# Taking the integer rounding of a normalised tile from eight compare-and-subtract rounds on one engine to eight relu/min rounds on two halves and two engines

## The reference, cut to what matters

```
xn    = layernorm(x)
query = xn@Wq ; key = xn@Wk ; value = xn@Wv
gq    = sum_s(query * softmax(query*SCALE))        # over the sequence
gk    = sum_s(p * softmax(p*SCALE)),  p = gq*key
attn  = query + (gk*value) @ Wr
ffn   = bitlinear(silu(bitlinear(xn, w_gate)) * bitlinear(xn, w_up), w_down)
out   = x + attn + ffn
_act_quant(x): scale = 127/max|x| per row; xq = clip(round(x*scale), -128, 127)/scale
_weight_quant(w): scale = 1/mean|w|; wq = clip(round(w*scale), -1, 1)/scale
```

## Time and profile before

| | us |
|---|---|
| median of 2 runs (5271.18 and 5273.79) | 5272.49 |
| profiled execution, its own time | 5271.05 |
| its span, first to last instruction, slowest core (the eight: 5258.3 to 5269.4) | 5269.4 |
| busy in the span: PE / DVE / ACT / POOL | 2267.0 / 3306.7 / 1899.7 / 60.7 |
| batch 0, after its first loads (125 to 640) | 515 |
| between the batches (640 to 796) | 156 |
| batch 1 (796 to 1378) | 582 |
| pass B (1378 to 1905) | 527 |
| gate/up stage (1905 to 4265) | 2360 |
| down projection (4265 to 5269) | 1004 |

### The profile page before, as it was taken

How to read it: one execution, slowest core, us unless ns; L and a number is a source line. 1 busy time by engine, 2 the same in 40 slices (tenths; PEclk the granted TensorE clock), 3 DMA queues, 4 the chain that set the end, 5 groups by cost and what they waited for, 6 DMA issues and landing times.

```text
span 5269.4 us, 37071 instructions; the slowest of 8 cores (5258.3 to 5269.4 us)
## 1 busy us (share of the span) xinstructions
PE 2267.0 (43%) x9998; PEld 1013.2 (19%) x10182; DVE 3306.7 (63%) x3647; ACT 1899.7 (36%) x2114; POOL 60.7 (1%) x117
## 2 busy tenths in 40 slices
PE   1443313433200043444444444444444406888888
PEld 0111101111100011211112111121111103444443
DVE  3777657777557767777777777777777731111111
ACT  1222213333100026555565655556555521111111
POOL 1000000000000000000000000000000000000000
PEclk9666656666555567767777677776767757888888
DMA  4222203333233310000000000000000032222221
GB/s 83 77 78 73 73 0 104 106 102 102 76 113 117 116 50 20 20 20 11 20 20 21 16 15 21 20 20 11 19 20 20 16 88 92 90 84 83 90 86 52
DMA packets 85712, 296.02 MB, mean 56 GB/s; under 512 B 9728, under 2 KB 9728, under 8 KB 77312
## 3 DMA queue, kind: packets, MB, share of 16 engines
q1 hardware_dynamic: 32256, 134.23, 7.3%
q10 hardware_dynamic: 39168, 117.46, 6.5%
q0 software_dynamic: 14080, 41.95, 3.1%
HBM read 209.72 MB, written 92.27 MB: 57 GB/s over the span
## 4 chain that ended last, share of the span: by engine, by line
DVE 38%; PE 27%; ACT 17%; issue 9%; DMA 7%; DVEq 1%; ACTq 1%; another core or an unknown queue 0%; POOL 0%; SPq 0%; POOLq 0%
ACT rA L666 10%; DVE fl L669 9%; PE PB L607 6%; DVE lh L360 6%; PE PC L610 6%; PE PA L807 4%; PE PC L807 4%; DVE lh L357 3%; PE PB L793 3%; DVE stat L628 3%; PE PT L777 2%; ACT z_hqT L781 2%; DVE fl L675 2%; DMA wdT_sb<-swdT 2%; ACT f_g L616 2%
## 5 line engine op out<-in xcount | busy, mean ns | idle before, releaser
L607 PE MATMUL PB<-wgT_sb,f_xiT 128*128 128x512 bf16 x1962 | 827.6, 422 | 1239.8 <-ACT f_g L616 1204.0
L666 ACT ACTIVATE rA<-fl,cbias 128x1024 bf16<-128x1024 f32 x512 | 588.1, 1149 | 440.0 <-DVE fl L656 284.9
L669 DVE SCALAR_TENSOR_TENSOR fl<-rA,fl 128x1024 f32<-128x1024 bf16 x512 | 627.2, 1225 | 163.2 <-ACT rA L666 162.9
L675 DVE SCALAR_TENSOR_TENSOR fl<-rB,fl 128x1024 f32<-128x1024 bf16 x512 | 625.0, 1221 | 15.1 <-ACT rB L672 13.0
L672 ACT ACTIVATE rB<-fl,cbias 128x1024 bf16<-128x1024 f32 x512 | 586.9, 1146 | 17.1 <-DVE fl L675 15.2
L607 PEld LDWEIGHTS PB<-wgT_sb,f_xiT 128*128 128x128 bf16 x2048 | 217.6, 106 | 1575.2 <-issue 1387.3
L610 PE MATMUL PC<-wuT_sb,f_xiT 128*128 128x512 bf16 x1024 | 468.0, 457 | 3.6 <-issue 2.4
L610 PE MATMUL PA<-wuT_sb,f_xiT 128*128 128x512 bf16 x1024 | 389.6, 380 | 18.3 <-DVE f_h L619 15.9
L616 ACT ACTIVATE f_g<-PB,cgv 128x512 f32<-128x512 f32 x256 | 168.0, 680 | 542.7 <-PE PC L610 530.8
L360 DVE TENSOR_TENSOR lh<-lh,lh 128x1024 f32<-128x1024 f32 x256 | 313.7, 1225 | 27.3 <-DVE lh L357 0.9
L470 PE MATMUL P<-p_w,p_rep 128*128 128x512 bf16 x62 | 36.3, 585 | 601.4 <-DVE p_w L467 553.9
(11 more groups left out here) (126 smaller groups left out, 3400.3 us busy)
## 6 DMA issues: line engine op xcount, KB each, us to landing
shqT<-f_hq SPq DMA_DIRECT2D x32, 1024.0 KB, 4.4
z_hq<-shqT SPq DMA_DIRECT2D x32, 1024.0 KB, 6.9
wf<-wgT ACTq DMA_DIRECT2D x48, 512.0 KB, 3.6
wf<-wuT ACTq DMA_DIRECT2D x48, 512.0 KB, 3.5
wf<-wdT ACTq DMA_DIRECT2D x48, 512.0 KB, 3.5
xbuf<-x SPq DMA_DIRECT2D x32, 512.0 KB, 4.1
sacc<-accs SPq DMA_DIRECT2D x32, 512.0 KB, 2.9
z_acc<-sacc ACTq DMA_DIRECT2D x32, 512.0 KB, 7.9
```

Of the source, the lines that this page charges most:

```text
L607: last = te.matmul(gps, lhsT, wgT_sb[:, k * I + jj * 512:k * I + (jj + 1) * 512], start=(k == 0), stop=(k == 7))
L666: o("scalar", (lambda j=j, scale=scale: lambda s: s.activation(rA[:], fl1[:], AF.Relu, scale=scale, bias=cbias[:, j:j + 1]))(), reads=[fl1 ...
L669: o("vector", (lambda cc=cc, op1=op1: lambda v: v.scalar_tensor_tensor(fl1[:], rA[:], cc, fl1[:], ALU.min, op1))(), reads=[rA_b], writes=[ ...
L675: o("vector", (lambda cc=cc, op1=op1: lambda v: v.scalar_tensor_tensor(fl2[:], rB[:], cc, fl2[:], ALU.min, op1))(), reads=[rB_b], writes=[ ...
```

## The change

In `stB` the rounding is rewritten, in the form that the gate/up stage has already. The tile is cut into two halves of 512 columns, lh1 and lh2, each made by a tensor_scalar of its own. A round is now, per half, a relu on ScalarE (2^40 times the difference to the power of two, so that the result is zero or very large; lrA or lrB, bf16) and a min-and-subtract on VectorE. The first round leaves the sum with its sign turned, so the later ones use the negative factor and add; in the end lh1 and lh2 hold minus the fraction. Two scalar_tensor_tensor make x*scale minus the fraction into xi16, and one tensor_scalar adds 0.5 in place. The biases `cbias` exist already (L255 to L258). The changed kernel's lines below this point lie 2 to 19 lower.

```diff
-    lh1, lh1_b = sb("lh1", [128, D], F32, 149.125)
-    lh2, lh2_b = sb("lh2", [128, D], F32, 153.125)
+    lh1, lh1_b = sb("lh1", [128, 512], F32, 149.125)
+    lh2, lh2_b = sb("lh2", [128, 512], F32, 151.125)
+    lrA, lrA_b = sb("lrA", [128, 512], BF16, 153.125)
+    lrB, lrB_b = sb("lrB", [128, 512], BF16, 154.125)
...
-        o("vector", (lambda t=t: lambda v: v.tensor_scalar(
-            lh1[:], xnf[:], svec[:, t:t + 1], 128.5, ALU.mult, ALU.add))(),
+        hA = xnf[:, 0:512]
+        hB = xnf[:, 512:1024]
+        o("vector", (lambda t=t, hA=hA: lambda v: v.tensor_scalar(
+            lh1[:], hA, svec[:, t:t + 1], 128.5, ALU.mult, ALU.add))(),
           reads=[xnf_b, svec_b], writes=[lh1_b])
-        for kb in range(7, -1, -1):
-            cc = float(2 ** kb)
-            o("vector", (lambda cc=cc: lambda v: v.tensor_scalar(
-                lh2[:], lh1[:], cc, cc, ALU.is_ge, ALU.mult))(),
-              reads=[lh1_b], writes=[lh2_b])
-            o("vector", lambda v: v.tensor_tensor(lh1[:], lh1[:], lh2[:], ALU.subtract),
-              reads=[lh2_b], writes=[lh1_b])
-        o("vector", (lambda t=t: lambda v: v.tensor_scalar(
-            lh2[:], xnf[:], svec[:, t:t + 1], 0.5, ALU.mult, ALU.add))(),
+        o("vector", (lambda t=t, hB=hB: lambda v: v.tensor_scalar(
+            lh2[:], hB, svec[:, t:t + 1], 128.5, ALU.mult, ALU.add))(),
           reads=[xnf_b, svec_b], writes=[lh2_b])
-        o("vector", lambda v: v.tensor_tensor(xi16[:], lh2[:], lh1[:], ALU.subtract),
-          reads=[lh2_b, lh1_b], writes=[xi16_b])
+        for j in range(8):
+            cc = float(2 ** (7 - j))
+            scl = (2.0 ** 40) if j == 0 else -(2.0 ** 40)
+            op1 = ALU.subtract if j == 0 else ALU.add
+            o("scalar", (lambda j=j, scl=scl: lambda s: s.activation(
+                lrA[:], lh1[:], AF.Relu, scale=scl, bias=cbias[:, j:j + 1]))(),
+              reads=[lh1_b, cbias_b], writes=[lrA_b])
+            o("vector", (lambda cc=cc, op1=op1: lambda v: v.scalar_tensor_tensor(
+                lh1[:], lrA[:], cc, lh1[:], ALU.min, op1))(),
+              reads=[lrA_b], writes=[lh1_b])
+            o("scalar", (lambda j=j, scl=scl: lambda s: s.activation(
+                lrB[:], lh2[:], AF.Relu, scale=scl, bias=cbias[:, j:j + 1]))(),
+              reads=[lh2_b, cbias_b], writes=[lrB_b])
+            o("vector", (lambda cc=cc, op1=op1: lambda v: v.scalar_tensor_tensor(
+                lh2[:], lrB[:], cc, lh2[:], ALU.min, op1))(),
+              reads=[lrB_b], writes=[lh2_b])
+        o("vector", (lambda t=t, hA=hA: lambda v: v.scalar_tensor_tensor(
+            xi16[:, 0:512], hA, svec[:, t:t + 1], lh1[:], ALU.mult, ALU.add))(),
+          reads=[xnf_b, svec_b, lh1_b], writes=[xi16_b])
...
+        o("vector", lambda v: v.tensor_scalar_add(xi16[:], xi16[:], 0.5),
+          reads=[xi16_b], writes=[xi16_b])
```

More of the change, by code:

```diff
@@ new lines, in stB @@
+        o("vector", (lambda t=t, hA=hA: lambda v: v.scalar_tensor_tensor(
+            xi16[:, 0:512], hA, svec[:, t:t + 1], lh1[:], ALU.mult, ALU.add))(),
+          reads=[xnf_b, svec_b, lh1_b], writes=[xi16_b])
+        o("vector", (lambda t=t, hB=hB: lambda v: v.scalar_tensor_tensor(
+            xi16[:, 512:1024], hB, svec[:, t:t + 1], lh2[:], ALU.mult, ALU.add))(),
+          reads=[xnf_b, svec_b, lh2_b], writes=[xi16_b])
+        o("vector", lambda v: v.tensor_scalar_add(xi16[:], xi16[:], 0.5),
+          reads=[xi16_b], writes=[xi16_b])
```

## The result

| | us |
|---|---|
| kernel before, median of 10 runs | 5291.93 |
| changed kernel, median of 13 runs | 5545.08 |
| ratio, 95% interval | 1.0461 (1.0415 to 1.0507) |
| profiled execution of the changed kernel, its own time | 5498.03 |
| predicted time and range | 5450 (5400 to 5500) |

The ratio leaves out runs in which one die ran at a lower granted clock, and the medians contain them, so the ratio and the profiled executions (5271.05 and 5498.03, +227 us) are what to compare. The changed kernel is slower, as forecast, by more than forecast: +227 us against +179. Its profiled execution lies 2 us inside the range; the ratio, 1.0461 x 5271 = 5514 us, and the median lie outside it.

What follows compares the result with a forecast made beforehand. VectorE was taken to bound both batches, with pass A hidden beside its rounding. Exposing pass A gave +39 us in batch 0 and +126, +18 and -4 in batch 1: +179 on 5271.05, so 5450 us, range 5400 to 5500.

Steps and rivals of the forecast that it cites:

- What bounds the kernel, and why pass A costs nothing there: Both batches: VectorE leads; pass A lies beside its 19.90 us rounding, with 6.22 us of cover left.
- The new rounding by itself: Rounding in the batches: a round takes 1.68 us, and VectorE saves 3.8 us per tile.
- The head: Start of the new rounding, a tensor_scalar of 512 columns on VectorE: 0.42 us.
- The tail: End of the rounding, after the last subtraction: second scalar_tensor_tensor 0.75 us, addition of 0.5 0.55 us; ends at about 16.1.
- What it moves: Batch steps: pass A's first load waits for the last relu, 15.4 us later; steps grow 2.8 and 9.66 us.
- The third term: Step path, pass A from first load issue to key copy: 8.7 us in batch 0, 15.6 in batch 1.
- The second term: Step path, from the rounding's start to the start of the last relu: 12.98 us.
- The sum: Whole kernel: +39 us in batch 0, +126, +18 and -4 in batch 1, together +179 us.
- The advice to keep relu on VectorE: Skill's rule for the rounding's relus: the swap loses by 1.66 times the time per element, whatever lies beside it.
- Hidden pass A: Rival, batch steps: pass A stays hidden and VectorE's gain comes through, -118 us, 5155 us; chance 0.03.
- Another table: Rival, ScalarE: relus need another table than Ln and Exp, +80 us on top, 5532 us; chance 0.03.
- Shrinking waits: Rival, pass A's loads: only a step's first sum waits, so +27 us, 5298 us; chance 0.04.

Runs made afterwards that it cites:

- run 4: Kernel before, with all 96 pieces of pass A moved out of the steps to behind batch 1; 5631.83 us.
- run 8: Kernel before, with pass A's loads issued two pieces ahead; ratio to the kernel before 0.9976.
- run 1: Changed kernel, with the store of the integer tile held back until the next step's sum x + query is written; median 5487.07 us, ratio 1.0404.
- run 3: Changed kernel, with all 96 pieces of pass A moved out of the steps to behind batch 1; 5552.55 us.
- run 7: Changed kernel, loads issued two pieces ahead, three pass A pieces a step in both batches, two behind the exponent, one behind the relus; ratio 0.9816.
- run 2: Changed kernel, with each of pass A's loads issued two pieces ahead, behind the sum that frees its buffer; median 5336.8 us, ratio 1.0122.

## Why the prediction was right or wrong

**What bounds the kernel, and why pass A costs nothing there: right.** Run 4, without pass A, and run 8, with early loads, leave the step at 35.24 to 35.27 us.

**The new rounding by itself: right in its rounds, short in its tail.** The relu has 0.722 us (0.72 expected), the subtraction 0.692 (0.69), a round is 1.68 us, and in most steps the last relu starts 12.97 us after the rounding's start (12.98). In 9 of 27 steps on core 7 it starts some 0.3 us later, which gives means of 13.12 in batch 0 and 13.05 in batch 1. The head has 0.49 (0.42) and the addition of 0.5 took 0.43 (0.55 taken, 0.25 to 0.75 the bounds). The tail left out an instruction: L378 (0.74 us) stands behind the last subtraction in VectorE's list too, and the prediction counted only the second of the two that make xi16. So the rounding lasts 16.52 us where no round is late, not 16.1, and VectorE gains 3.4 us per tile, not 3.8. This cost the sum nothing, since the tail lies beside pass A.

**What it moves: right.** The load is issued when the last relu starts, the step's path is reciprocal, rounding, pass A, key copy, exponent; VectorE waits at the reciprocal 15.6 to 17.8 us in batch 1 (15 predicted) and 8.3 to 9.7 in batch 0 (8). The gap from key copy to reciprocal is 1073.56 - 1069.54 = 4.02 us (4.04).

**The third term, pass A from first issue to key copy, was sized too small, and this is the step that failed.** The four terms of a step, as means over the steps 3 to 16 of batch 0 and 3 to 15 of batch 1, from the timelines of two cores of the changed kernel:

| us | reciprocal to rounding | to last relu | pass A | key copy to reciprocal | step |
|---|---|---|---|---|---|
| batch 0, predicted | 12.31 | 12.98 | 8.7 | 4.04 | 38.0 |
| batch 0, core 7 (slowest) | 12.33 | 13.12 | 9.42 | 4.04 | 38.90 |
| batch 0, core 6 (fastest) | 12.33 | 13.12 | 8.98 | 4.04 | 38.46 |
| batch 1, predicted | 12.31 | 12.98 | 15.6 | 4.04 | 44.9 |
| batch 1, core 7 | 12.37 | 13.05 | 17.24 | 4.02 | 46.68 |
| batch 1, core 6 | 12.37 | 13.05 | 16.49 | 4.02 | 45.93 |

The other three terms stand. Pass A was put 0.72 and 1.64 us too low for the slowest core; over 14 and 15 steps this makes 10 + 25 = 35 of the 48 us that are missing. The second term adds 3 us, the first reciprocal of batch 0 came 4 us later on this core (131.82 instead of 127.62), and 6 us lie behind the last reciprocal of batch 1, in stages that the change does not touch. Three things are in the 35:
- *In batch 1 the row came from a core with short loads.* Core 6 was the slowest before, when nothing of its loads counted. Its mean from issue to sum in batch 1 was 3.60 us, the lowest of the eight; their mean was 3.74 and the highest 3.86. (In batch 0, from step 2 on, core 6 had 3.80 against a mean of 3.72, so this does not explain batch 0.) In the changed kernel core 6 is the fastest of all, and the slowest core decides:

```profile
core 6: 5471.0 us, clock 0.701
core 7: 5496.4 us, clock 0.702
```

- *The store of the integer tile runs into the second load*, +0.4 us, which run 1 took away: 12 us over the two batches.
- *A rest of 0.08 to 0.15 us per load* over all cores, which run 1 left. The order of the step alone does not make it: run 3 has 0.17 us per load more than run 4 where both run pass A behind the batches, and in pass B, which the change does not touch, the loads of wgT and wuT that GpSimd issues land after 4.08 to 4.23 us in all seven runs with the new rounding, against 3.83 to 3.98 in the three without (means of eight cores). What makes the loads slower in these programs stays open.

About half of the 35 us is already there on core 6 itself (0.28 and 0.89 us a step, 17 us), the other half is the step from core 6 to core 7. I had allowed 0.3 us on each of 88 pieces, 26 us, which is less than that, and nothing for the slowest core being another one.

**The sum:** +39 us in batch 0 became 14 x (38.90 - 35.24) = +51; +126 for steps 3 to 15 of batch 1 became 13 x (46.68 - 35.27) = +148. Steps 0 to 2 of batch 1 with the stretch before them, last reciprocal to first, grew from 213.3 to 233.7 us, +20 for the +18 of steps 1 and 2, and step 16 of batch 1 lost 3.75, for 3.8.

**The advice to keep relu on VectorE** (the Trainium skill, ScalarE: Activation LUTs, Rules for kernel authors): the sign of the result agrees with it, but not for its reason, which is VectorE's speed per element. Runs 3 and 4 show the swap gaining 3.3 us per step where nothing else stands in ScalarE's list.

**The rivals.** *Hidden pass A*: refuted by the issue at 1052.02 and by 363.1 us of waiting; run 7 hides pass A by another order, at 5191 us against the 5155 reckoned for it. *Another table*: refuted; the groups of the changed kernel have the same two loads as the earlier trace rows, 1.283 us each. *Shrinking waits*: refuted, they grew (batch 1, before each sum: 151.5/60 = 2.53 us before, 181.6/60 = 3.03 after).

## What to carry to other kernels

Before work goes from a busy engine to an idle one, read the idle engine's list, not its busy share: here ScalarE was 31% busy (179.90 of 582 us), but 151.5 us of its idle time were waits for loads issued just ahead of their use, and that waiting was free only while it stood beside the other engine's long stretch. Put such fillers, loads first, where the engine waits for something else; the same relus then gain 1.8% (run 7) instead of losing 4.6%. When a transfer that was hidden comes onto the path, size it from all cores and add what will run beside it in the new order: the slowest core decides, and while the transfer is hidden the slowest core need not be the one with the slowest transfers.

## What was not expected of the hardware

- Two 512 KB loads in flight at once took 3.83 and 5.55 us from issue to their sums (run 2); one at a time took 3.6 to 3.9 (means of the eight cores before, batch 1).
- A 256 KB store issued close to a 512 KB load (on core 7 mostly within 0.5 us) goes with a longer way of that load to its sum: 4.24 us in the changed kernel and 3.81 with the store held back (mean of eight cores, batch 1). The store itself had a median of 2.3 us to landing before, and in the changed kernel (DMA issues of the page: count, size, median us to landing):

```profile
sxi<-xi POOLq DMA_DIRECT2D x32, 256.0 KB, 4.5
```

  In run 3, with no pass A in the steps, it was back at 2.3. Held back in run 1 it took 5.4, and the loads of x, whose median had been 4.1, took 4.8; the collision went to other transfers, which nothing waited for in the steps.
- In run 7 the loads of x took a median of 8.6 us to landing instead of 4.1, and the step was still VectorE's own 31.9.
- Across cores the differences are reproducible only in part: core 6 was the fastest in both profiled executions of the changed kernel (5471.0 and 5470.9 us), and cores 1 and 7 were at 5495 or above both times, but core 0 had 5496.0 in one and 5473.2 in the other.
